# Cross-attention of a perceiver block: low parts moved by the sync engine's transfers, scaled scores and running maximum one step later, once-a-batch steps earlier in VectorE's queue

## The reference

```
x   = x + xattn(ctx_768, layernorm(x), mask)      # 8 batches, 64 queries, 1601 context rows of 192, 4 heads of 64
x   = x + attn(layernorm(x))                      # an rwkv6 recurrence
x   = x + ffn(layernorm(x))                       # 16 experts, top 4, and a shared one

xattn: xn, ln = layernorm(ctx), layernorm(latents)
       q = ln Wq;  k, v = concat(xn Wkv, ln Wlkv)       # keys: 1601 context rows and the 64 latents
       attn = softmax(rmsnorm(q) * scale . rmsnorm(k), context masked)
       out  = (attn . v) Wo + bo
```

## Time and profile before

| | us |
|---|---|
| median of 3 runs | 519.65 (518.51 to 521.28) |
| the profiled execution, its own time | 514.96 |
| its span | 513.2 |
| first row maximum / eighth row maximum | 82.2 / 318.7 |
| TensorE, VectorE, GpSimd, ScalarE busy | 427.2, 402.1, 244.7, 239.1 |
| granted TensorE clock, mean | 0.967 of full speed |

### The profile page before, as it was taken

The page is one execution under the profiler, slowest core; times in us unless marked ns, Lnnn a source line. Parts: engine busy times, 40 slices in busy tenths (PEclk is TensorE's granted clock), DMA queues, the critical chain, the costliest instruction groups (busy, mean ns, idle before and its releaser), DMA issues.

```text
span 513.2 us, 6607 instructions
## 1 busy us (share of the span) xinstructions
PE 427.2 (83%) x2042; PEld 332.5 (65%) x2042; DVE 402.1 (78%) x969; ACT 239.1 (47%) x547; POOL 244.7 (48%) x248
## 2 busy tenths in 40 slices
PE   3786758788889878978989969887997789789996
PEld 0363535567767766867767758764374667568885
DVE  5846789999999999999988896425569556887776
ACT  0237744556575656755556535321242115335551
POOL 6351866658458465584575542001521331445550
PEclk9998978989999999999999999899999986999999
DMA  8604932040141131403100002910000000000001
GB/s 247 186 1 138 251 129 66 2 142 2 52 142 52 26 119 52 140 4 121 29 3 1 2 0 79 406 40 0 0 2 0 1 0 0 1 1 1 0 2 42
DMA packets 23975, 31.80 MB, mean 62 GB/s; under 512 B 2954, under 2 KB 19652, under 8 KB 23940
## 3 DMA queue, kind: packets, MB, share of 16 engines
q1 hardware_dynamic: 23940, 31.38, 19.8%
HBM read 30.69 MB, written 0.52 MB: 61 GB/s over the span
## 4 chain that ended last, share of the span: by engine, by line
DVE 42%; PE 29%; POOL 15%; issue 10%; ACT 2%; DMA 1%; SPq 1%; DVEq 0%; POOLq 0%; ACTq 0%
PE bank L571 27%; POOL kr L481 10%; DVE kss L1406 6%; DVE arena L1418 5%; DVE arena L1454 5%; DVE split_b L1397 5%; DVE cst L1343 3%; DVE arena L1613 2%; POOL crs L447 2%; DVE arena L1627 1%; DVE kguard L1409 1%; DVE big L1328 1%; DVE cmv L1347 1%; DMA mask_in<-in_p_mask 1%; DVE split_b L1687 1%
## 5 line engine op out<-in xcount | busy, mean ns | idle before, releaser
L571 PE MATMUL bank<-keyq,split_b 128*128 128x512 f32 (+2 forms) x724 | 168.4, 380 | 21.4 <-DVE split_b L1687 7.5
L571 PEld LDWEIGHTS bank<-keyq,split_b 128*128 128x128 f32 (+1 forms) x724 | 123.0, 192 | 52.3 <-issue 19.0
L481 POOL TENSOR_TENSOR kr<-kguard,neg_half 128x8 f32<-128x8 f32 (+1 forms) x56 | 93.3, 1666 | 104.6 <-DVE kguard L1409 104.4
L571 PE MATMUL bank<-arena 128*128 128x193 f32 (+4 forms) x528 | 100.0, 332 | 8.4 <-DVE arena L1613 4.4
L571 PEld LDWEIGHTS bank<-arena 128*128 128x128 f32 (+2 forms) x528 | 85.6, 192 | 18.2 <-issue 13.0
L1130 ACT ACTIVATE arena<-bank 128x512 f32<-128x512 f32 (+1 forms) x56 | 31.6, 563 | 73.4 <-PE bank L571 72.8
L571 PE MATMUL bank<-split_b,keyq 128*128 128x512 f32 x204 | 51.8, 405 | 0.0
L1397 DVE TENSOR_TENSOR split_b<-arena,split_b 32x256 fp32r<-32x256 f32 (+1 forms) x112 | 47.5, 424 | 2.5
L1418 DVE TENSOR_TENSOR arena<-bank,kr 128x512 f32<-128x512 f32 (+1 forms) x56 | 36.0, 643 | 15.3 <-POOL kr L481 15.1
L571 PEld LDWEIGHTS bank<-split_b,keyq 128*128 128x128 f32 x204 | 39.1, 197 | 7.7
L470 POOL TENSOR_TENSOR split_b<-arena,split_b 128x256 fp32r<-128x256 f32 (+1 forms) x56 | 38.4, 685 | 8.9 <-ACT split_b L1105 8.8
(11 more groups left out here) (221 smaller groups left out, 613.5 us busy)
## 6 DMA issues: line engine op xcount, KB each, us to landing
arena<-in_ctx SPq DMA_DIRECT2D x16, 576.0 KB, 4.2
arena<-in_p_ctxT SPq DMA_DIRECT2D x8, 800.5 KB, 6.4
arena<-in_p_ctxT SPq DMA_DIRECT2D x8, 400.2 KB, 7.1
arena<-in_p_experts SPq DMA_DIRECT2D x1, 2688.0 KB, 18.4
arena<-in_p_experts SPq DMA_DIRECT2D x1, 2304.0 KB, 12.1
arena<-in_p_experts SPq DMA_DIRECT2D x1, 1536.0 KB, 6.5
X<-in_x SPq DMA_DIRECT2D x1, 512.0 KB, 3.7
arena<-in_t_Wlkv SPq DMA_DIRECT2D x1, 512.0 KB, 6.9
```

What stands on the lines that cost most here:

```text
L481: pool.tensor_tensor(kr[0:r, n % 2, 0:k], kg_[0:r, n % 2, 0:k], neg_half[0:r, 0:4 * k].rearrange("p (t h) -> p t h", h=H), ALU.pow).then_i ...
L571: return nc.tensor.matmul(out_, l, r, start=start, stop=stop, skip_group_check=shared)
```

## The change

1. `split_side` on VectorE is gone. GpSimd's `split_rest` computes the low part of all 64 channels in one instruction into a new buffer `side_low` (two slots), and SP moves it in two transfers of 32 partitions into rows 96 to 127 of `xs` (`move_side`). `keys(n)` waits for the transfers (`side_in`) in place of `xs_side`.
2. In VectorE's queue, `norm_scores` and `running_max` of group u-1 stand in step u; they come ahead of `group_stats`.
3. `evac_latent_out` comes ahead of `key_sums`, `refold_low_part` right behind it; ScalarE's `twin` after a refold is done in step 1 and not in step 0.
4. GpSimd's `context_scales` is done in one piece a batch, in step 2.
5. SP's queue is a loop over steps: the pair of `move_side(u + 2)` first; the first half of the context in step 0, the two parts of the turned context in steps 1 and 2, `spread_sd` and then the second half of the context in step 4; the 19 weight transfers one a step from step 14 on, `wx2a` in step 35.

```diff
+        side_low = sb("side_low", [SMALL, 2, 256], F32R)
...
+            def move_side(n):
+                k = 256 if n % NG < NG - 1 else TAIL
+                sp.wait_ge(xs_side, n + 1)
+                for j in range(2):
+                    sp.dma_start(xs[n % 3][96:P, 2 + j, 0:k].bitcast(F32), side_low[32 * j:32 * j + 32, n % 2, 0:k].bitcast(F32)).then_inc(side_in[n % 3], 16)
...
+            move_side(0)
+            move_side(1)
+            for u in range(groups):
+                b, g = divmod(u, NG)
+                if u + 2 < groups:
+                    move_side(u + 2)
+                if g == 0 and b + 2 < B:
...
                     load_context(b + 2, 0)
-                if b + 1 < B:
-                    load_turned(b + 1)
-                if b + 2 < B:
+                if g in (1, 2) and b + 1 < B:
+                    load_turned(b + 1, g - 1)
+                if g == 4 and b + 1 < B:
+                    spread_sd(b + 1)
+                if g == 4 and b + 2 < B:
                     if b + 2 >= 4:
                         sp.wait_ge(y_part, NG * (b - 1))
                     load_context(b + 2, 1)
+                if 2 * NG <= u < 2 * NG + len(mixer_weights):
+                    dst, src = mixer_weights[u - 2 * NG]
+                    sp.dma_start(dst, src).then_inc(mixer_in, 16)
...
-            def context_scales(b, part):
-                pool.wait_ge(caggr, 2 * b + part + 1)
+            def context_scales(b):
+                pool.wait_ge(caggr, 2 * b + 2)
...
+                then(pool.tensor_tensor(crs[:, k], cve[:, k], neg_half[:, 0:FULL + 1], ALU.pow))
...
                 pool.tensor_tensor(v[:, 1, 0:k], raw[:, 0], v[:, 0, 0:k].bitcast(F32), ALU.subtract).then_inc(xs_rest, 1)
+                pool.wait_ge(xs_small, n + 1)
+                if n >= 2:
+                    pool.wait_ge(side_in[(n - 2) % 3], 32 * ((n - 2) // 3 + 1))
+                pool.tensor_tensor(side_low[:, n % 2, 0:k], raw[0:SMALL, 1], v[0:SMALL, 2, 0:k].bitcast(F32), ALU.subtract).then_inc(xs_side, 1)
...
-                pe.wait_ge(xs_side, n + 1)
+                pe.wait_ge(side_in[n % 3], 32 * (n // 3 + 1))
...
+                if g == 1 and 2 <= b <= 5:
+                    act.wait_ge(refold_high, b - 1)
+                    twin((b + 2) % 4 + 1, (b + 2) % 4 + 2)
...
+                if g == 4 and 2 <= b <= B + 1:
+                    evac_latent_out(b - 2)
                 if u < groups:
                     key_sums(u)
+                if g == 0 and 2 <= b <= 5:
+                    refold_low_part(b + 2)
                 if g == 3 and 2 <= b <= B + 1:
                     evac_sum(b - 2)
-                if g == 4 and 2 <= b <= B + 1:
-                    evac_latent_out(b - 2)
...
-                if u + 2 < groups:
-                    split_side(u + 2)
+                if 0 <= u - 1 < groups:
+                    norm_scores(u - 1)
+                    running_max(u - 1)
                 if u + LEAD < groups:
                     group_stats(u + LEAD)
-                if u < groups:
-                    norm_scores(u)
-                    running_max(u)
-                if g == 0 and 2 <= b <= 5:
-                    refold_low_part(b + 2)
```

More of the change, by code:

```diff
@@ L349, in _ @@
             sp.wait_ge(pool_const, 1)
-            load_turned(0)
+            mixer_weights = (
+                    (wo[:], a["t_Wo"].rearrange("(c p) n -> p c n", p=P)),
+                    (bo[:], a["L0_xattn_bo"].rearrange("(o d) -> o d", o=1)),
+                    (sums[:], a["c_sums"]), (pick[:], a["c_pick"]), (headsel[:], a["c_head"]),
+                    (wx0[:], a["t_W_x0"].rearrange("(c p) n -> p c n", p=P)),
+                    (wx2b[:], a["t_W_x2"][P:160, :]),
+                    (wr[:], a["t_W_r"].rearrange("(c p) n -> p c n", p=P)),
+                    (wk[:], a["t_W_k"].rearrange("(c p) n -> p c n", p=P)),
+                    (ww1[:], a["t_W_w1"].rearrange("(c p) n -> p c n", p=P)),
+                    (ww2[0:64, :], a["t_W_w2"]), (ww2[64:65, :], a["L0_attn_b_w2"].rearrange("(o d) -> o d", o=1)),
+                    (wv[:], a["t_W_v"].rearrange("(c p) n -> p c n", p=P)),
+                    (wg[:], a["t_W_g"].rearrange("(c p) n -> p c n", p=P)),
+                    (wo2[:], a["t_W_o"].rearrange("(c p) n -> p c n", p=P)),
+                    (gatew[:], a["t_gate_w"].rearrange("(c p) n -> p c n", p=P)),
+                    (ebias[:], a["L0_ffn_e_bias"].rearrange("(o d) -> o d", o=1).broadcast_to([P, NE])),
+                    (before[:], a["c_before"].broadcast_to([P, NE * NE])),
+                    (gbefore[:], a["c_gbefore"].broadcast_to([P, 16])),
+            )
+            for c in range(2):
+                load_turned(0, c)
             load_context(1, 0)
@@ L368, in _ @@
                     load_context(b + 2, 1)
[L369 to L388, removed]
+                if 2 * NG <= u < 2 * NG + len(mixer_weights):
+                    dst, src = mixer_weights[u - 2 * NG]
+                    sp.dma_start(dst, src).then_inc(mixer_in, 16)
+                if u == 5 * NG:
                     sp.wait_ge(wx2_zero, 1)
@@ L486, in _ @@
             then(pool.memset(wx2a[:], 0.0))
-            context_scales(0, 0)
-            context_scales(0, 1)
+            context_scales(0)
             latent_rms(0)
@@ L498, in _ @@
                 if g == 2 and b + 1 < B:
-                    context_scales(b + 1, 1)
+                    context_scales(b + 1)
                 if g == 4 and b + 1 < B:
@@ L502, in _ @@
                 key_scales(u)
-                if g == 0 and b + 1 < B:
-                    context_scales(b + 1, 0)
                 if u == 0:
@@ L1077, in refold_high_part @@
                 last.then_inc(refold_high, 1)
-                act.wait_ge(refold_high, b - 3)
-                twin(b % 4 + 1, b % 4 + 2)
             def twin(lo, hi):
@@ L1388, in refold_low_part @@
                 last.then_inc(refold_low, 1)
-            def split_side(n):
-                b, g = divmod(n, NG)
-                dve.wait_ge(xs_small, n + 1)
-                k = 256 if g < NG - 1 else TAIL
-                v, side_ = xs[n % 3], ctxT[b % 2][:, 1, 256 * g:256 * g + k]
-                for j in range(2):
-                    last = V.tensor_tensor(v[96:P, 2 + j, 0:k], side_[32 * j:32 * j + 32], v[32 * j:32 * j + 32, 2 + j, 0:k].bitcast(F32), ALU.subtract)
-                last.then_inc(xs_side, 1)
             def key_sums(n):
@@ L1535, in _ @@
                 fold_low_part(j)
-            split_side(0)
-            split_side(1)
             for n in range(NG, LEAD):
```

29 lines of the change are left out of this document (11 added, 18 removed).

## The result

The changed kernel takes 498.75 us (median of 4 runs, 497.62 to 501.73) against 519.37 for the kernel before in the same runs: ratio 0.961 [0.9585, 0.964]. The prediction was 501.5, in 490 to 513. Size and sign were right. How the sum comes to it was not: its largest term is worth less than nothing, and an edit that it priced at nothing carries more of the gain than any other.

A forecast was written before the change was run, and what follows sets the result against it. VectorE's queue was taken to set the pace, some 4 us a batch above TensorE's need. Gains of 9.9, 2.0, 3.2, 3.0 and 0.7 less 0.7 made 18.1 us: 501.5 us, own range 496 to 507, eight in ten 490 to 513.

The forecast's parts named there:

- VectorE stops being the bound, TensorE takes over: Middle batches: without split_side VectorE falls to 26.0 us a batch, and TensorE's 30.4 is the bound.
- By it moving the subtraction changes which one waits, not the sum: VectorE instructions with two SBUF inputs contend with GpSimd's SBUF reads; moving the subtraction was to leave the total unchanged.
- Scores and maximum one step later ... No wait: VectorE's norm_scores and running_max of group u-1 in step u: no wait expected, 0.7 us cost at the loop's end.
- They release exactly the waits of the earlier trace: 9.7 + 6.7: Moving refold_low_part and evac_latent_out ahead releases TensorE's waits at L709 and L755: 16.4 us in five batches.
- One `context_scales` a batch: GpSimd, one step a batch: 1.3 us more ahead of key_scales and the next low part, charged whole each batch.
- The transfers: SP's pair moving each low part takes 2.9 us; hidden, with 3.2 us spare before TensorE waits.
- The slower rival: 10%: the pair lands after 10.0 us behind the turned context in SP's queue, once in seven batches; 529 us.
- The middle: Five middle batches: 16.4 us from released waits less 5 x 1.3 for the scales, a gain of 9.9 us.
- the last batch: Batch 286.6 to 318.7 us: gain of 2.0 us, with -0.7 at the end of the loop.
- The two batches ahead and the start: Gains of 3.2 us in batch 82.2 to 114.9, 3.0 in the first batch and 0.7 at the start.
- GpSimd didn't become the bound (22%): 22% rival: GpSimd instructions held by VectorE's make it need 33 us a batch, so the kernel takes 510 us.

The follow-up runs named there:

- the halves: The changed kernel with context_scales in two parts again, 6 columns behind key_scales in step 0 and 7 in step 2: 491.94 us, ratio 0.950.

## Why the prediction came out right, and where it was wrong

*VectorE stops being the bound, TensorE takes over:* right. The busy time of a middle batch was put at 26.0 us for VectorE and is 28.4 (141.97 / 5); 1.7 of the 2.4 us are the disturbed shifts and guards. GpSimd's was put at 26.1 and is 25.5. The batch itself was put at 32 to 32.5 us and is 32.8, with the granted clock at 0.95, where the prediction had 1.00 from the earlier trace rows. "By it moving the subtraction changes which one waits, not the sum" was the sentence that failed there: `split_side` on VectorE ran longer at times beside a power; its successor on GpSimd makes two of every three shifts of VectorE longer, and some of the guards.

*"Scores and maximum one step later ... No wait":* this is the step that failed most. The argument was only that the delay does no harm. It was not asked what the scores would wait for without it, once `split_side` and its 0.85 us no longer stood between the sums and the scores. The trace already had it: VectorE waits 5.5 us for the power in the batch where its queue is short, which the prediction quotes, but also 5.0 us in 12 times in the five middle batches and 4.5 in the two ahead of them. These the prediction didn't count, though it called VectorE the engine that sets the pace. Where the work that covers a wait leaves, the wait has to be charged to the kernel without the cover. What the delay is worth is 11.0 us in the old kernel and 23.3 in the new.

*"They release exactly the waits of the earlier trace rows: 9.7 + 6.7":* the waits went, and not by the moves; the kernel with the steps in their old places is 7.9 us faster. The wait was put down to the place of the step, while it was VectorE's load that made the step late. A wait in the trace of before says who was late, not that his place in the queue is why.

*One `context_scales` a batch:* the charge of 6.5 us (five times 1.3) is near the 6.8 measured, and that is luck. GpSimd was to eat into the spare of the low parts; it is the transposes of `csd` (L655) that wait, and about half of what the halves give back in the middle batches is busy time of TensorE at a higher clock, which the charge didn't contain.

*The transfers:* right in the middle batches, where TensorE never waits for one. A single transfer lands 1.8 us after its issue (median); for a pair 2.9 were taken, and the two pairs for which TensorE visibly waits need 2.5 and 2.6 us from the first issue until it goes on. These waits, 2.6 and 4.1 us, fall in the first batch. The slower rival (10.0 us behind the bulk loads) didn't come, though what the transfers cost in all is known only to within some 11 us. VectorE does wait for the context's second half, 4.3 us in three times, out of its own slack.

*Batch by batch.* The terms went wrong with opposite signs. The middle was to give 9.9 us and gives 7.4; the last batch 1.3 with the end of the loop, and the stretch from 284.0 gives 6.0: TensorE's idle time in it fell from 8.3 to 3.5 us, and of VectorE's 5.5 us for the power nothing is left. The two batches ahead and the start were to give 6.9 and give 4.6, 2.0 of it by the first cut. That the later parts lose 1.6 us was not foreseen. The forecast of 18.1 us stands against 16.4 between the two profiled executions. That it is so near is partly luck.

*The rivals.* GpSimd didn't become the bound (22%), but the mechanism named for it, two engines holding each other's instructions, is there: shifts and guards run longer, and 8 of 26 splits take 0.82 to 1.17 us and not 0.73. The condition was a GpSimd at 33 us a batch; it has 25.5 busy and idles between.

Not settled: the moves' 7.9 us are shown in total, but `refold_low_part` and `evac_latent_out` were not tried apart. Of the 19.1 us of GpSimd's subtraction, the runs don't divide disturbed neighbours, its own place in the chain and the clock. SP's new order and the later `twin` were never undone by themselves, so their share is not known.

## What to carry to other kernels

Ask of every wait in the profile whether it is there because of where the waiting-for step stands or because its engine is full; only the first goes with a move, and a move in a queue that is about to empty has nothing to win and can delay what it is put ahead of. When work leaves an engine, look at what that work was covering. And weigh a subtraction moved to GpSimd with its neighbours: here it cost 0.73 us there undisturbed (0.81 in the mean), 0.48 on VectorE in one instruction, and lengthened VectorE's shift in two steps of three besides.

## What the runs showed of the hardware

**A short idle time followed by half the clock.** In the changed kernel TensorE waits 1.58 us for `csd` at 122.08. The timeline around it (start, us), then windows across it (granted clock third from the end):

```profile
117.87 2.63 PE L586 MATMUL bank<-keyq,split_b 128*128 128x512 f32 x10
...
118.78 2.89 POOL L461 TENSOR_TENSOR crs<-cve,neg_half 128x13 f32<-128x13 f32 x1
...
122.08 0.28 PE L655 MATMUL bank<-ident,csd 128*13 128x128 f32 x1 [1.58 <-POOL csd L464]
...
124.70 4.63 PE L586 MATMUL bank<-keyq,split_b 128*128 128x512 f32 x10
```

```profile
122.00:123.40 1.40, 1.32 (x9) 1.10 (x9) 0.25 (x2) 1.00 (x5) 1.40 (x2) 0.94 0.89 211
123.40:130.00 6.60, 6.60 (x19) 5.41 (x20) 4.71 (x12) 1.61 (x6) 5.16 (x7) 0.50 0.30 93
130.00:134.00 4.00, 4.00 (x23) 3.53 (x23) 3.77 (x9) 2.08 (x6) 2.35 (x2) 0.99 0.54 154
```

For 6.6 us the granted clock is 0.50 (1.2 GHz), and the same ten products take 4.63 us instead of 2.63. The stretch costs more than the idle time ahead of it. In the kernel before the middle batches run at 1.00 throughout, though TensorE idles up to 2.8 us at L709. And in the changed kernel itself L655 waits for `csd` in each of the five middle batches: 1.58 or 1.59 us at 122.08, 155.91, 188.14 and 219.71, 0.95 at 253.81. Four are followed within 3 us by a stretch at half clock (6.6 us long, then some 3.4 us each); the one at 188.14 is not. So the length of an idle time alone doesn't decide it; what does is open, and that the waits bring the stretches about is likely and not shown. In these batches TensorE's busy time rose by the 4.3 us named above.

**GpSimd's subtraction costs the same for half the rows:** undisturbed, 64x256 takes 0.72 to 0.74 us, as 128x256 does, and their means in the middle batches are 0.81 and 0.82. So cutting rows from this instruction bought nothing; on VectorE the same 64x256 took 0.48.
